# Decoder block on one core: queries and keys evicted by whole banks, parts moved within SBUF, engine step orders rewritten

## The reference, cut to what matters

```python
q = jnp.einsum('bxy,iyk->bxik', x, Wq).reshape(h, b, t, hs)
k = jnp.einsum('bxy,iyk->bxik', x, Wk).reshape(h, b, t, hs)
v = jnp.einsum('bxy,iyk->bxik', x, Wv).reshape(h, b, t, hs)
wei = jnp.einsum('hbqd,hbkd->hbqk', q, k) * hs ** (-0.5)
wei = jnp.where(causal, wei, -jnp.inf)
out = jnp.einsum('hbqk,hbkd->hbqd', jax.nn.softmax(wei, axis=-1), v)
out = out.reshape(b, t, h * hs) @ proj_w.T + proj_b
```

## Time and profile before

| | |
|---|---|
| median of 3 runs | 1594.37 us (1593.98 to 1594.75) |
| the profiled execution, its own time | 1595.14 us |
| its span | 1593.3 us |
| PE busy | 1371.1 us (86%) |
| DVE busy | 1229.9 us (77%) |
| ACT busy | 996.5 us (63%) |
| POOL busy | 730.3 us (46%) |
| mean granted clock of TensorE | 0.943 |

### The profile page before, as it was taken

The page is one execution under the profiler, slowest core; times in us unless marked ns, Lnnn a source line. Parts: engine busy times, 40 slices in busy tenths (PEclk is TensorE's granted clock), DMA queues, the critical chain, the costliest instruction groups (busy, mean ns, idle before and its releaser), DMA issues. The chain is left out here.

```text
span 1593.3 us, 49653 instructions
## 1 busy us (share of the span) xinstructions
PE 1371.1 (86%) x17623; PEld 1146.9 (72%) x17623; DVE 1229.9 (77%) x3308; ACT 996.5 (63%) x2381; POOL 730.3 (46%) x921
## 2 busy tenths in 40 slices
PE   4699999999999999999999999752699999999940
PEld 3587888788788878877887888641488888888830
DVE  4789999999999999999989989737555555555538
ACT  4667877788878778878878867521444444444426
POOL 2135445555564575565555634411143333433326
PEclk9799999999999999999999999965699999999975
DMA  6545444444434444343444323008511411111136
GB/s 176 139 130 140 130 133 122 112 132 128 119 94 146 121 113 129 120 128 100 137 126 116 114 73 83 18 8 329 204 48 49 156 46 46 49 51 47 48 111 219
DMA packets 138892, 178.80 MB, mean 112 GB/s; under 512 B 78782, under 2 KB 110654, under 8 KB 134176
## 3 DMA queue, kind: packets, MB, share of 16 engines
q1 hardware_dynamic: 127616, 153.71, 32.3%
q0 software_dynamic: 6816, 17.71, 3.6%
q10 hardware_dynamic: 4224, 4.19, 0.7%
HBM read 93.79 MB, written 65.93 MB: 100 GB/s over the span
## 5 line engine op out<-in xcount | busy, mean ns | idle before, releaser
L1564 PE MATMUL ps_e<-xt,wres 128*128 128x128 f16 x3408 | 354.4, 220 | 0.5 <-issue 0.3
L1564 PEld LDWEIGHTS ps_e<-xt,wres 128*128 x3408 | 287.7, 98 | 72.9 <-issue 1.3
L1620 ACT ACTIVATE act_g<-ps_e,b 128x128 f32<-128x128 f32 x568 | 162.0, 368 | 224.7 <-PE ps_e L1564 116.7
L1571 PE MATMUL ps_e<-wres,g_hi 128*128 x568 | 214.5, 379 | 1.3 <-DVE g_lo L1650 1.3
L649 ACT ACTIVATE probs<-st_k,nmax 128x128 f32<-128x128 f32 (+1 forms) x512 | 200.6, 449 | 7.3 <-DVE nmax L842 5.2
L1523 POOL DMA_INDIRECT z_scr<-e_y,dst_i x71 | 84.4, 1188 | 219.6 <-DVE e_y L1641 219.6
L842 DVE CUSTOM_DVE_ANT_0 st_k<-ps,causal 128x128 f32<-128x128 f32 (+1 forms) x512 | 160.2, 349 | 6.9 <-PE ps L391 5.8
L399 PE MATMUL ps<-ident,probs 128*128 128x128 f32 x768 | 131.8, 281 | 31.8 <-ACT probs L649 20.5
L847 DVE TENSOR_TENSOR pt_lo<-ps,pt_hi 128x384 f16<-128x384 f32 x256 | 141.6, 553 | 19.4 <-ACT pt_hi L656 17.6
L1573 PE MATMUL ps_e<-wres,g_lo 128*128 x568 | 154.8, 273 | 0.0
L656 ACT ACTIVATE pt_hi<-ps 128x384 f16<-128x384 f32 x256 | 124.5, 486 | 45.3 <-PE ps L416 38.3
(11 more groups left out here) (249 smaller groups left out, 4423.5 us busy)
## 6 DMA issues: line engine op xcount, KB each, us to landing
st_p<-in_moe_w SPq DMA_DIRECT2D x24, 768.0 KB, 5.7
w_scr<-st_p SPq DMA_DIRECT2D x24, 768.0 KB, 4.1
wres<-w_scr SPq DMA_DIRECT2D x18, 1024.0 KB, 21.8
v_scr<-v_tok SPq DMA_DIRECT2D x32, 512.0 KB, 2.6
v_pos<-v_scr SPq DMA_DIRECT2D x32, 512.0 KB, 4.4
k_pair<-k_pair SPq DMA_DIRECT2D x32, 512.0 KB, 4.6
z_scr<-zero SPq DMA_DIRECT2D x32, 256.0 KB, 3.5
wres<-z_scr SPq DMA_DIRECT2D x8, 1024.0 KB, 13.7
```

The costliest lines, as they stand in the source:

```text
L1564: last = mm(out, w(c * FF + f * P, b, P), xt[:, t % 2, a, c], start=(m == 0), stop=(m == 5))
L1571: mm(out[:, 0:2 * D], g_hi[:, t % G_BUFS, f], w(KC * FF + f * D, 0, 2 * D), start=(f == 0), stop=False, skip_group_check=True)
L1620: nc.scalar.activation(act_g[:, k % 2, f], ps[:, 3 + 2 * (k % 2) + f // 4, (f % 4) * P:(f % 4 + 1) * P], ACT.Gelu, bias=bias[:, f:f + 1], ...
```

## The change

Queries and keys are laid out anew, with heads 0 to 7 and heads 8 to 15 as two blocks of a group of 8 tokens. Each fill of queries and keys is evicted by one operation on ACT and one on DVE, over 128 partitions x 512; the parts that then lie on the wrong partitions are moved by DMAs within SBUF (`key_move`, `key_double`, `query_move`, `query_low`). The low part of the queries goes to a buffer of its own first. Values are written to scratch in two blocks and read by two DMAs; their positions within a group follow the new order, as do the mask and the turning of the outputs (whose columns are put back in order as they are written to PSUM). `other_weights` is issued right behind the first weights. The mask is built as an fp16 pattern on POOL, multiplied by 32768 on PE into PSUM, and copied twice by ACT. The norm's two semaphores become one. All engines' lists are rewritten.

```diff
-V_LOADS = 1
-
-
-OPS_BEFORE = [sum(1 if kind == "v" else 2 for kind, _ in FILLS[:j]) for j in range(NF + 1)]
-NOPS = OPS_BEFORE[NF]
-V_OPS = OPS_BEFORE[3]
-K_OPS = OPS_BEFORE[4]
+V_LOADS = 2
+
+V_FILLS, K_FILLS = 3, 4
...
-    q_st = sb("q_st", [P, 2, P, H], F16)
-    k_pair = sb("k_pair", [P, 2, 2, P, H], F16)
+    q_st = sb("q_st", [P, 2, 2 * GROUPS, 2, GTOK // 2, PAIRS], F16)
+    q_low = stage["q"][:, 0, 0:P * PAIRS // 2].bitcast(F16).rearrange("p (b t i) -> p b t i", t=GTOK // 2, i=PAIRS)
+    k_pair = sb("k_pair", [P, 2, 2, 2, P, PAIRS], F16)
...
+    ident_big, causal16 = (sm_shift[:].rearrange("p h k -> p (h k)").bitcast(F16)[:, n * P:(n + 1) * P] for n in range(2))
...
         def v_out(t):
...
-            sp.dma_start(io["v_scr"][p], v_tok[:, p].rearrange("p h k d -> p (h k d)")).then_inc(s_v_out, 16)
+            sp.dma_start(v_places[p].rearrange("(a b t i e) -> (b t) a (i e)", a=2, b=2 * GROUPS, t=GTOK // 2, i=PAIRS),
+                         v_tok[:, p].rearrange("p (a i) k d -> p a (i k d)", a=2)).then_inc(s_v_out, 16)
         def v_in(t):
             p = t % 2
             sp.wait_ge(s_v_out, 16 * (t + 1))
...
                 sp.sem_inc(s_held_sp, 1)
             if t == 0:
                 sp.wait_ge(s_one, 2)
-            sp.dma_start(v_pos[:, p, :, 1:1 + 2 * HS],
-                         io["v_scr"][p].rearrange("(g t) (h e) -> (t h) g e", t=GTOK // 2, h=H)).then_inc(s_v_in, 16)
+            for a in range(2):
+                sp.dma_start(v_pos[a * HS:(a + 1) * HS, p, :, 1:1 + 2 * HS],
+                             v_places[p].rearrange("(a b n e) -> a n b e", a=2, b=2 * GROUPS, n=HS)[a]).then_inc(s_v_in, 16)
+        def key_move(t):
+            p = t % 2
+            sp.wait_ge(s_fill_lo, NF * t + K_FILLS)
+            sp.sem_inc(s_held_sp, 1)
+            sp.dma_start(k_pair[0:HS, p, :, 1], k_pair[HS:P, p, :, 0]).then_inc(s_kmove, 16)
+            sp.dma_start(k_pair[HS:P, p, :, 1], k_pair[HS:P, p, :, 0]).then_inc(s_kmove, 16)
+
         def key_double(t):
             p = t % 2
-            sp.wait_ge(s_fill_lo, NOPS * t + K_OPS)
+            sp.wait_ge(s_kmove, 32 * (t + 1))
             sp.sem_inc(s_held_sp, 1)
-            sp.dma_start(k_pair[HS:P, p], k_pair[0:HS, p]).then_inc(s_kdup, 16)
+            sp.dma_start(k_pair[HS:P, p, :, 0], k_pair[0:HS, p, :, 0]).then_inc(s_kdup, 16)
+
+        def query_move(t):
+            p = t % 2
+            sp.wait_ge(s_fill_hi, NF * (t + 1))
+            sp.sem_inc(s_held_sp, 1)
+            sp.dma_start(q_st[0:HS, p, :, 1], q_st[HS:P, p, :, 0]).then_inc(s_qmove, 16)
+
+        def query_low(t):
+            p = t % 2
+            sp.wait_ge(s_fill_lo, NF * (t + 1))
+            sp.sem_inc(s_held_sp, 1)
+            sp.dma_start(q_st[HS:P, p, :, 1], q_low[HS:P]).then_inc(s_qlow, 16)
+            sp.wait_ge(s_qmove, 16 * (t + 1))
+            sp.dma_start(q_st[HS:P, p, :, 0], q_low[0:HS]).then_inc(s_qlow, 16)
...
                 first_weights()
+                other_weights()
             if s >= 0 and has(s + 2):
                 load_x(s + 2)
             if has(s + 1):
                 v_out(s + 1)
                 v_in(s + 1)
+                key_move(s + 1)
+                key_double(s + 1)
             if has(s):
                 load_rows(s)
             if has(s) and even(s):
                 load_context(half(s))
             if has(s + 1):
-                key_double(s + 1)
+                query_move(s + 1)
+                query_low(s + 1)
...
-            if s == -1:
-                other_weights()
...
-                pe.wait_ge(s_fill_lo, NOPS * t + (OPS_BEFORE[j - 1] if j else OPS_BEFORE[NF - 1] - NOPS))
+                pe.wait_ge(s_fill_lo, NF * t + j - 1)
...
+        def keys(p, low, b, n):
+            size = GTOK // 2 * PAIRS
+            k = k_pair[:, p, low].rearrange("p a t i -> p a (t i)")[:, :, b * size:(b + n) * size]
+            return k if n == 1 else k.rearrange("p a (b n) -> p b a n", b=2)
+
         def scores(t, g):
             p = t % 2
             if t == 0 and g == 0:
                 pe.wait_ge(s_const, N_CONST)
             if g == 0:
-                pe.wait_ge(s_fill_lo, NOPS * (t + 1))
                 pe.wait_ge(s_kdup, 16 * (t + 1))
+                pe.wait_ge(s_qlow, 32 * (t + 1))
             if since(t, 1) or g:
                 pe.wait_ge(s_max, 2 * (GROUPS * t + g))
-            qs, kh, kl = (m[:, g * GTOK:(g + 1) * GTOK].rearrange("p t h -> p (t h)")
-                          for m in (q_st[:, p], k_pair[:, p, 0], k_pair[:, p, 1]))
-            mm(ps_s[:, 0:P], qs[:, 0:P], kh[:, 0:P], start=True, stop=False, skip_group_check=True)
-            mm(ps_s[:, 0:P], qs[:, 0:P], kl[:, 0:P], start=False, stop=True, skip_group_check=True)
-            mm(ps_s[:, P:384], qs[:, P:256], kh[:, :], start=False, stop=False, skip_group_check=True)
-            last = mm(ps_s[:, P:384], qs[:, P:256], kl[:, :], start=False, stop=True, skip_group_check=True)
+            q_first, q_second = (q_st[:, p, 2 * g + b].rearrange("p a t i -> p (a t i)") for b in range(2))
+            mm(ps_s[:, 0:P], q_first, keys(p, 0, 2 * g, 1), start=True, stop=False, skip_group_check=True)
+            mm(ps_s[:, 0:P], q_first, keys(p, 1, 2 * g, 1), start=False, stop=True, skip_group_check=True)
+            mm(ps_s[:, P:384], q_second, keys(p, 0, 2 * g, 2), start=False, stop=False, skip_group_check=True)
+            last = mm(ps_s[:, P:384], q_second, keys(p, 1, 2 * g, 2), start=False, stop=True, skip_group_check=True)
             last.then_inc(s_scores, 1)
...
+        pe.wait_ge(s_const, N_CONST)
+        mm(c7[:, 0:P], ident_big, causal16, start=True, stop=True).then_inc(s_const, 1)
         run(step)
...
-            to = q_st[:, p] if kind == "q" else k_pair[:, p, 0]
-            for a in range(2):
-                src = ps_a[j % 2][a * HS:(a + 1) * HS].rearrange("p (h t) -> p t h", h=4)
-                nc.scalar.activation(to[0:HS, :, PAIRS * a + 4 * n:PAIRS * a + 4 * n + 4], src, ACT.Copy).then_inc(s_fill_hi, 1)
+            src = ps_a[j % 2]
+            if kind == "q":
+                nc.scalar.activation(q_st[:, p, :, 0, :, 4 * n:4 * n + 4], src.rearrange("p (h b t) -> p b t h", h=4, t=GTOK // 2),
+                                     ACT.Copy).then_inc(s_fill_hi, 1)
+            else:
+                nc.scalar.activation(k_pair[:, p, 0, 0, :, 4 * n:4 * n + 4], src.rearrange("p (h t) -> p t h", h=4), ACT.Copy).then_inc(s_fill_hi, 1)
...
+        act.wait_ge(s_const, N_CONST + 1)
+        for n in (0, 2):
+            nc.scalar.activation(causal[:, n], c7[:, 0:P], ACT.Copy).then_inc(s_const, 1)
         run(step)
...
-            high = (q_st[:, p] if kind == "q" else k_pair[:, p, 0])[0:HS]
-            low = q_st[HS:P, p] if kind == "q" else k_pair[0:HS, p, 1]
-            for a in range(2):
-                dve.wait_ge(s_fill_hi, NOPS * t + OPS_BEFORE[j] + a + 1)
-                at = slice(PAIRS * a + 4 * n, PAIRS * a + 4 * n + 4)
-                src = ps_a[j % 2][a * HS:(a + 1) * HS].rearrange("p (h t) -> p t h", h=4)
-                stt(out=low[:, :, at], in0=src, scalar=1.0, in1=high[:, :, at], op0=ALU.mult, op1=ALU.subtract).then_inc(s_fill_lo, 1)
+            dve.wait_ge(s_fill_hi, NF * t + j + 1)
+            at = slice(4 * n, 4 * n + 4)
+            if kind == "q":
+                if n == 0 and since(t, 1):
+                    dve.wait_ge(s_qlow, 32 * t)
+                nc.vector.tensor_tensor(q_low[:, :, :, at], ps_a[j % 2].rearrange("p (h b t) -> p b t h", h=4, t=GTOK // 2),
+                                        q_st[:, p, :, 0, :, at], ALU.subtract).then_inc(s_fill_lo, 1)
+            else:
+                stt(out=k_pair[:, p, 1, 0, :, at], in0=ps_a[j % 2].rearrange("p (h t) -> p t h", h=4), scalar=1.0,
+                    in1=k_pair[:, p, 0, 0, :, at], op0=ALU.mult, op1=ALU.subtract).then_inc(s_fill_lo, 1)
...
-                nc.gpsimd.affine_select(out=m[:], in_=m[:], compare_op=ALU.not_equal, fill=1.0, base=0,
+            for m, one in ((ident, 1.0), (ident16, 1.0)):
+                nc.gpsimd.affine_select(out=m[:], in_=m[:], compare_op=ALU.not_equal, fill=one, base=0,
                                         pattern=[[-1, P]], channel_multiplier=1).then_inc(s_const, 1)
-            for n in (0, 2):
-                nc.gpsimd.affine_select(out=causal[:, n], in_=causal[:, n], compare_op=ALU.is_ge, fill=MASKED, base=0,
-                                        pattern=[[-1, P]], channel_multiplier=1).then_inc(s_const, 1)
+            places = [[-PAIRS, 2], [-H, GTOK // 2], [-1, PAIRS]]
+            nc.gpsimd.affine_select(out=ident_big, in_=ident_big, compare_op=ALU.not_equal, fill=32768.0, base=0,
+                                    pattern=places, channel_multiplier=1).then_inc(s_const, 1)
```

More of the change, by code:

```diff
@@ L533, in step @@
                 turn_probs(s, 0)
-                scores(s, 2)
             if has(s + 1):
-                fill(s + 1, 2)
-            if has(s - 2):
-                pv2(s - 2, 1)
```

(34 more changed lines are left out.)

244 lines of the change are left out of this document (118 added, 126 removed).

## The result

The changed kernel takes 1608.72 us (median of 5 runs, 1603.0 to 1614.71), the kernel before 1594.75 beside it (5 runs, 1593.98 to 1597.81). The ratio is 1.0081, with a 95% interval of 1.0051 to 1.0112. It is slower by 0.8%; the forecast was 1565 us, with a range of 1538 to 1589. The profiled execution took 1610.21 us (span 1608.5).

A forecast was written before the change was run, and what follows sets the result against it. PE and DVE were both over 91% busy, with PE stopping at five places per step. 1595.1 - 21.7 (steps) - 8 (start) = 1565.4, 0.8 less for the median: 1565 us, range 1538 to 1589.

The forecast's parts named there:

- the wait for x_lo: PE's stop for POOL's low half of the tokens, 0.43 us per step, was to go since POOL splits earlier.
- the router matmul 1.25 us by the walk: New PE stop after the cross scores, before the router matmul or the sixth turn, put at 1.25 us per step.
- a step above 31 us: Sign that the forecast is wrong; the forecast step was 30.4 us against 31.06 before.
- The rival of late queries: Next tile's scores wait for query moves landing 9.2 us after the eviction: 2.2 us per step, 1655 us; chance 0.08.
- I cost the queue at nothing; the bound is one late weight piece, 1 us per step: Transfers behind the added moves on SyncE were to cost nothing; at worst 1 us per step for 24 steps.
- I take the middle, 0.7 us per step: Steps' gain between 0.2 by places and 1.2 by walking the engines: 0.7 us, 21.7 us over 31 steps.
- The sum over places: PE's stops per step added up: 2.3 us in the new order against 2.5 before, a gain of 0.2.
- The walk's closing time of 29.9: One step followed through all engines' new orders ended after 29.9 us, a gain of 1.2, leaving out small gaps.
- Nearest row 4.4: Landing time of the old values in, 2048 pieces of 256 bytes, 4.4 us, used to price the last query moves.
- 8 us go: At the start, ACT's 8.16 us stop for projection weights was to vanish by asking for them behind the first weights.
- the same time, bound 3 either way: First scores were to stay at 31.68 us: evictions end 1.3 earlier, query moves take 4.8; bound 3 us.
- a reordered chain that costs 0.5 more per step: Rival for the steps: new engine orders lengthen a chain by 0.5 us per step, 1603 us; chance 0.04.

The follow-up runs named there:

- kernels with unchanged steps: The changed kernel and two edits of it that touch only its start (late weights late again; keys and queries ahead of values): steps 31.25 to 31.41 us.
- the kernel with three edits: Changed kernel with ACT's weight-piece split later, values in by one transfer, and keys and queries ahead of values at the start: 1585.46 us.
- router later: Changed kernel with PE's router matmul moved from right behind its turn to behind fill 0 and pv 4: 1608.33 us.
- the turn's subtraction first: Router matmul behind fill 0 and pv 4, DVE's pt 4 ahead of predicated copies and maximum: 1668.76 us on the changed kernel, 1657.00 with three further edits.
- the kernel with a stop of 2.5 us in each step: Changed kernel with the PE, ACT, DVE and POOL lists of the kernel before: 1677.71 us.
- that with a stop of 1.7 us: Changed kernel with the router matmul behind fill 0 and pv 4 and DVE's pt 4 ahead of predicated copies and maximum: 1668.76 us.

## Why the prediction was wrong

The forecast was 21.7 us less in the steps and 8 less at the start. The profile has 10.6 more in the steps and 4.0 more at the start. So 32 us of the miss lie in the steps and 12 at the start.

**Right.** The evictions' prices and the relief of DVE and ACT; the wait for x_lo gone; the places of the new waits: the router matmul 1.25 us by the walk, 1.01 as idle time; the cross scores 0.45 against 0.47; the eighth turn 0.3, where 0.37 from start to start of matmuls include 0.13 of the one ahead; no steady wait for a query transfer. Of its signs of being wrong one came, a step above 31 us. The rival of late queries, 128-byte pieces too slow, is refuted: 13 ns a piece, 3.1 us to landing. So the Trainium skill's sentence on 512 bytes (DMA: Bandwidth & Descriptors, Specifications) did not decide here. The exception that the Trainium skill makes for transfers within SBUF (the same page, Why small descriptors are slow) agrees in the main: a 128-byte piece moves at 9.8 bytes per ns and a 2048-byte piece of the keys, 134 ns, at 15.3.

**The step, first cause: "I cost the queue at nothing; the bound is one late weight piece, 1 us per step".** It was the bound. In ACT's new list the split of the weight piece stands ahead of stage_d 1, exps 2 and pt 1, which came before it in the old one. SyncE asks for the piece half a microsecond after POOL's third part in both kernels, but it now lands in 6.4 us and not 5.7, and ACT stands 1.3 us for it in every step. The walk had ACT in its new order and no such stop. With the piece later on ACT the time falls by 13.4 us between the medians and by 10.8 by the two ratios, where the steps had lost 10.6; between the profiles the step is 0.55 us shorter, and against the kernels with unchanged steps at least 0.4.

**The step, second cause: "I take the middle, 0.7 us per step".** Two sums contradicted each other. The sum over places gave 0.2, and with the late piece out of the way the step gains about that: 31.06 to 30.86, and 30.88 in the kernel with three edits. The walk's closing time of 29.9 had left out the small gaps; half of the gap between a sum and a model that omits known terms is no estimate. That the sum came out is in part luck. With the piece later PE idles 41.5 us in 19 steps, more than the 37.1 before; what fell is its busy time, from 553.3 to 545.7. It now stops three times per step and not five, and by the prediction's 0.15 us for each stop's drained pipeline that is 0.3 us per step of the 0.4. Less work on DVE and ACT, together with the new orders, was thus worth 0.2 us per step and not 0.7.

The 0.2 is a small difference of two large effects. With the old evictions the new lists make the step 33.5 us long, 2.4 more than before; the relief, the moves and the later piece take 2.6 off again. So the lists that were written to use the relief used it up: PE's waits come from a chain through three engines (cross scores, predicated copies, subtraction, turn, and behind them the evictions for the fills), and taking single links out of that chain (router later, the turn's subtraction first) moved the stop or made it longer. What the relief is worth with the old lists stays open, since there PE waits for the query move.

**The transfers.** "Nearest row 4.4" was taken for values in as well. Their two transfers go to 64 partitions each, and a 256-byte piece then takes 39 ns and not 18. The trace before had a hint: the old key copy, to 64 partitions, took 634 ns for a piece of 8192 bytes in the packets' records, where 4096 bytes of values out took 159. Undoing it is worth some 6 us of the changed kernel's time; how much of it lies in the steps is not shown.

**The start: "8 us go", "the same time, bound 3 either way".** The stop of 8.16 us did go. But the first scores came 15 us later. The prediction put 4.8 us of query moves behind the eviction and nothing ahead of them in the queue. In truth four landings lie one behind the other: values out 8.6 us, the key moves 7.5, and two of the query moves, 3.9 and 2.9. In steady steps a whole step covers them, at the start nothing does. Undoing the early weights gives 5.5 us of the 15, and the chain is 9.5. The first projection is only 4.0 us later: the stop that went gives back 8 of the 15, and the other 3 were not traced. The clock gave nothing back either, 0.82 over the start where it had been 0.85.

The prediction's one rival by way of this queue was placed at the query moves in the steps, where it had itself counted 6.3 us of cover; the start, where nothing covers them, had none. The nearest of its rivals in time, "a reordered chain that costs 0.5 more per step" at 1603 us, had a chance of 0.04 and named no chain.

**What is left open.** The exact share of the small gaps in the steps was not tried. Nor was a start with the late weights between the first tile's moves, or a third place of the router matmul together with a later one of the low query parts. Why values out and the key moves land later in the steps is seen only beside the weight piece's new distance, and no run moves that alone.

## What to carry to other kernels

Relief on an engine that is not the bound is worth what its chain puts before the bound, no more: count the places where the bound engine stands, and believe that sum over one that leaves out terms. When a transfer is added, walk the whole issuing queue for the first tile, where nothing covers it, and ask for each old transfer when it is now issued and when it is now wanted: here an untouched one, the weight piece, cost most. Orders and prices belong together: the new lists with the old evictions cost 76 us, the old lists with the new ones 84, and moving one subtraction ahead of 1.6 us of work cost 60. And where a change brings longer stops of TensorE, read the granted clock as well: in the last two cases between a third and a half of the steps' loss was busy time at the lower level.

## What the runs showed of the hardware

A piece of 256 bytes from HBM took 39 ns in the median when a transfer went to 64 partitions, and 18 when it went to 128, with the same number of pieces, and 18 again in two transfers over all partitions. Other sizes were not compared like with like: 2048-byte pieces within SBUF over 64 partitions took 134 ns, 8192-byte ones 634. Pieces of 128 bytes within SBUF over 64 partitions took 13 ns, and a move of 1024 of them landed in 3.1 us. An operation of ACT or DVE on 128 partitions took what it took on 64 (595 and 681 ns for 512 columns, against 589 and 689).

In the kernel with a stop of 2.5 us in each step (up to 3.7) the granted clock was 0.96 of full over 19 steps, and in that with a stop of 1.7 us it was 0.97, with short stretches at 0.50 behind the stops; in the changed kernel, whose longest steady stop is 1.0 us, it stayed at 1.00. It was 1.00 as well with the new orders alone, where PE idled more in all, 4.5 us per step, but in eight places of at most 1.3 us.
